# Gated linear attention: gate scan one step later, a third x buffer, and a reordered prologue

## What is computed

```python
q = feature_map((x @ Wq.T) * SCALE); k = feature_map(x @ Wk.T); v = x @ Wv.T   # 16 heads of 16
gate = sigmoid(x @ Wg.T + bg)                                                  # one per token and head
def step(S, inp):
    q_t, k_t, v_t, g_t = inp
    S = g_t[:, :, None, None] * S + k_t[..., :, None] * v_t[..., None, :]
    y_t = einsum('bhi,bhij->bhj', q_t, S)
    return (S, y_t)
y = scan(step)                                                                 # over 1024 tokens
x = layernorm(x + y @ Wo.T)
```

## Time and profile before

| | us |
|---|---|
| runs of the kernel before | 1459.67, 1451.2, 1449.83 |
| their median | 1451.2 |
| the profiled execution, its own time | 1458.73 |
| its span, first to last instruction | 1456.9 |
| mean granted TensorE clock, as a share of full speed | 0.966 |
| PE busy / DVE busy / ACT busy over the whole span | 1357.9 / 790.0 / 582.5 |

### The profile page before, as it was taken

The page is one execution under the profiler, slowest core; times in us unless marked ns, Lnnn a source line. Parts: engine busy times, 40 slices in busy tenths (PEclk is TensorE's granted clock), DMA queues, the critical chain, the costliest instruction groups (busy, mean ns, idle before and its releaser), DMA issues. The chain is left out here.

```text
span 1456.9 us, 22495 instructions
## 1 busy us (share of the span) xinstructions
PE 1357.9 (93%) x7690; PEld 861.7 (59%) x7691; DVE 790.0 (54%) x1539; ACT 582.5 (40%) x1280; POOL 299.8 (21%) x345
## 2 busy tenths in 40 slices
PE   7888999889999999999999997889999999899996
PEld 4555666665555566666666664446665564577774
DVE  4887888866443122222222222467778656676764
ACT  5466666752110122222222221144443532566665
POOL 1133333311673000000000001622220000234343
PEclk9898999979999999999999999899999999999998
DMA  4654555729221011111111112313110000000001
GB/s 143 210 191 167 194 194 195 236 72 347 104 101 50 22 47 47 43 43 47 47 43 43 45 48 62 109 36 98 29 30 0 1 0 12 0 1 16 29 16 58
DMA packets 76741, 115.83 MB, mean 80 GB/s; under 512 B 10032, under 2 KB 62576, under 8 KB 72560
## 3 DMA queue, kind: packets, MB, share of 16 engines
q1 hardware_dynamic: 70096, 97.89, 20.3%
q0 software_dynamic: 6144, 16.79, 3.6%
q10 hardware_dynamic: 416, 0.03, 0.0%
HBM read 82.86 MB, written 31.82 MB: 79 GB/s over the span
## 5 line engine op out<-in xcount | busy, mean ns | idle before, releaser
L1698 POOL DMA_INDIRECT m_got<-outs,slot x64 | 61.2, 956 | 562.1 <-DMA outs<-XT 454.1
L1103 DVE TENSOR_TENSOR ro_h<-ro_bB,ro_sl 128x512 f32<-128x512 f32 x71 | 49.1, 692 | 220.3 <-PE ro_bB L1052 220.3
L548 DVE TENSOR_TENSOR_SCAN a_dcy<-a_gbc,a_ident 128x2048 f32<-128x2048 f32 x32 | 141.6, 4425 | 4.6 <-DMA a_gbc<-gd 0.9
L2054 POOL TENSOR_TENSOR q_hr<-q_hf,q_hr 128x512 fp32r<-128x512 f32 x64 | 83.5, 1315 | 287.6 <-ACT q_hr L1895 287.6
L1047 PE MATMUL ro_bA<-Win,ro_xT 128*128 x284 | 136.4, 603 | 0.8 <-ACT ro_xT L1074 0.6
L1059 PE MATMUL ro_bO<-Wout,ro_hT 128*128 x568 | 134.3, 379 | 0.9 <-DVE ro_hT L1096 0.9
L1059 PEld LDWEIGHTS ro_bO<-Wout,ro_hT 128*128 128x128 f32 x568 | 107.8, 190 | 45.6 <-issue 34.6
L1052 PE MATMUL ro_bB<-Wsw,ro_xT 128*128 x284 | 134.7, 597 | 0.0
L1083 ACT ACTIVATE XT<-ro_bO 128x256 f32<-128x256 f32 x71 | 27.3, 384 | 204.9 <-PE ro_bO L1059 204.9
L1096 DVE COPY ro_hT<-ro_bH 128x512 f32<-128x512 f32 x71 | 49.1, 692 | 101.3 <-PE ro_bH L1032 101.3
L1052 PEld LDWEIGHTS ro_bB<-Wsw,ro_xT 128*128 128x128 f32 x284 | 54.6, 192 | 69.0 <-issue 69.0
(11 more groups left out here) (270 smaller groups left out, 2519.1 us busy)
## 6 DMA issues: line engine op xcount, KB each, us to landing
a_gbc<-gd SPq DMA_DIRECT2D x32, 1024.0 KB, 5.7
rows<-a_zero SPq DMA_DIRECT2D x8, 1152.0 KB, 8.9
XT<-rows SPq DMA_DIRECT2D x71, 128.0 KB, 2.0
outs<-XT SPq DMA_DIRECT2D x71, 128.0 KB, 1.7
a_xt<-in_xTt SPq DMA_DIRECT2D x8, 512.0 KB, 3.8
X<-in_x SPq DMA_DIRECT2D x8, 512.0 KB, 7.5
Win<-in_w_in SPq DMA_DIRECT2D x8, 512.0 KB, 10.5
Wsw<-in_w_sw SPq DMA_DIRECT2D x8, 512.0 KB, 10.4
```

The lines of the kernel that those rows point to most:

```text
L548: v.tensor_tensor_scan(dcy[:, :], gbc[j % 2][:, :], ident16[:, :], 0.0, ALU.mult, ALU.add).then_inc(d_done, 1)
L1698: pool.indirect_dma_start(out=got[q % 2][k][:, t, :], out_offset=None, in_=mem["outs"], in_offset=bass.IndirectOffsetOnAxis(ap=slot[:, k, ...
L2054: pool.tensor_tensor(hr[:, 1, f % 4, :], hf[f % 2][:, :], hr[:, 0, f % 4, :], ALU.subtract).then_inc(hl_done, 1)
```

## The change

The DVE's `gate_decay(n // 4 + 1)` moves from steps n % 4 == 0 to steps n % 4 == 1, and on SP the `gates_out` and `decays_out` of that chunk move with it, now behind `gates_in` and `decays_in` of the step. x has three buffers instead of two, so `load_x(T)` waits for work on chunk T-3 to end instead of T-2 and stands in another place on SP. In the prologue the two fills that PE's opening matmuls read come first on DVE, those matmuls wait for these two fills alone and are 5 instead of 8, and `decay(0)` runs after `phi(1)` instead of after `phi(3)`.

```diff
-        xt = [sb(f"xt{p}", [P, G, B * P]) for p in range(2)]
+        xt = [sb(f"xt{p}", [P, G, B * P]) for p in range(3)]
...
                 def load_x(T):
-                    if T >= 2:
-                        sp.wait_ge(v_ready, 4 * (T - 1))
-                        sp.wait_ge(z_ready, T - 1)
-                    sp.dma_start(xt[T % 2][:, :, :], io["xTt"][T]).then_inc(xt_in[T % 2], 16)
+                    if T >= 3:
+                        sp.wait_ge(v_ready, 4 * (T - 2))
+                        sp.wait_ge(z_ready, T - 2)
+                    sp.dma_start(xt[T % 3][:, :, :], io["xTt"][T]).then_inc(xt_in[T % 3], 16)
...
                 for n in range(0, NT):
-                    if n % 4 == 0 and n // 4 + 1 < NC:
-                        gates_out(n // 4 + 1)
-                        decays_out(n // 4 + 1)
                     if n + 2 < NT:
                         gates_in(n + 2)
                     if 4 <= n + 2 < NT:
                         decays_in(n + 2)
-                    if n % 4 == 2 and n // 4 + 2 < NC:
-                        load_x(n // 4 + 2)
+                    if n % 4 == 1 and n // 4 + 1 < NC:
+                        gates_out(n // 4 + 1)
+                        decays_out(n // 4 + 1)
+                    if n == 0:
+                        load_x(2)
+                    if n % 4 == 3 and n // 4 + 3 < NC:
+                        load_x(n // 4 + 3)
...
+                pe.wait_ge(init, 2)
+                for _ in range(5):
+                    pe.matmul(bV[:, 0:D], zeros[:, :], zero[:, :], start=True, stop=True)
                 pe.wait_ge(init, 3)
-                for _ in range(8):
-                    pe.matmul(bV[:, 0:D], zeros[:, :], zero[:, :], start=True, stop=True)
...
             def _(v):
+                v.memset(zeros[:, :], 0.0).then_inc(init, 1)
+                v.memset(zero[:, :], 0.0).then_inc(init, 1)
                 for t in vz:
...
-                v.memset(zero[:, :], 0.0).then_inc(init, 1)
-                v.memset(zeros[:, :], 0.0).then_inc(init, 1)
...
-                    if n >= 0 and n % 4 == 0 and n // 4 + 1 < NC:
+                    if n >= 0 and n % 4 == 1 and n // 4 + 1 < NC:
                         gate_decay(n // 4 + 1)
...
-                    if tile(n + 1):
+                    if tile(n + 1) and n >= 0:
                         decay(n + 1)
...
                     if Q < 4:
                         phi(Q)
+                    if Q == 1:
+                        decay(0)
```

More of the change, by code:

```diff
@@ L124, in build_attention @@
             sem(k) for k in ("init", "wg_in", "wqk_in", "wv_in", "wo_in", "cst_in", "x_in", "ex_in"))
-        xt_in, gb_in = [sem("xt_in0"), sem("xt_in1")], [sem("gb_in0"), sem("gb_in1")]
+        xt_in, gb_in = [sem(f"xt_in{p}") for p in range(3)], [sem("gb_in0"), sem("gb_in1")]
         gd_out, ed_out = sem("gd_out"), sem("ed_out")
@@ L241, in project @@
                     if o == 0:
-                        pe.wait_ge(xt_in[T % 2], 16 * (T // 2 + 1))
+                        pe.wait_ge(xt_in[T % 3], 16 * (T // 3 + 1))
                     if Q == 0:
@@ L249, in project @@
                     for g in range(G):
-                        mm = pe.matmul(projected(Q), Wqk[:, g, o * P:(o + 1) * P], xt[T % 2][:, g, :], start=(g == 0), stop=(g == G - 1))
+                        mm = pe.matmul(projected(Q), Wqk[:, g, o * P:(o + 1) * P], xt[T % 3][:, g, :], start=(g == 0), stop=(g == G - 1))
                     mm.then_inc(qk_ready, 1)
                 def gates(T):
-                    pe.wait_ge(xt_in[T % 2], 16 * (T // 2 + 1))
+                    pe.wait_ge(xt_in[T % 3], 16 * (T // 3 + 1))
                     if T == 0:
@@ L258, in gates @@
                         for g in range(G):
-                            mm = pe.matmul(bY[32 * b:32 * b + 32, Z0:Z0 + P], WgT[:, g, :], xt[T % 2][:, g, b * P:(b + 1) * P],
+                            mm = pe.matmul(bY[32 * b:32 * b + 32, Z0:Z0 + P], WgT[:, g, :], xt[T % 3][:, g, b * P:(b + 1) * P],
                                            start=(g == 0), stop=(g == G - 1))
@@ L271, in values @@
                     for g in range(G):
-                        mm = pe.matmul(bV[:, 0:D], xt[T % 2][:, g, b * P:(b + 1) * P], Wv[:, g, :], start=(g == 0), stop=(g == G - 1))
+                        mm = pe.matmul(bV[:, 0:D], xt[T % 3][:, g, b * P:(b + 1) * P], Wv[:, g, :], start=(g == 0), stop=(g == G - 1))
                     mm.then_inc(v_ready, 1)
```

## The result

The changed kernel takes 1431.16 us (median of four runs, 1429.67 to 1432.45), the kernel before 1452.48 us (1449.83 to 1459.67): a ratio of 0.984, 95% interval 0.9813 to 0.9868. The forecast was 1421, range 1409 to 1439, with 0.85 on faster. The profiled execution took 1432.45 us in place of 1458.73, 26.3 us less.

A forecast was written before the change was run, and what follows sets the result against it. Bound: in attention, DVE's 26.6 us of waits for ACT's sigmoid of the gates. Gains of 26.0 (chunks) and 6.6 (prologue) sum to 32.6; 28.6 to 32.6 off the 1451.2 median gives 1421 us, range 1409 to 1439.

The forecast's parts named there:

- detour of 3.08 us: ACT's table loads around the sigmoid in gate steps: stays, costs PE 0, with 3.08 a chunk as far end.
- Rival 1: ACT becomes the bound in gate steps, its table detour landing on PE: 1439 in full, 1430 for half; chance 0.14.
- rival 3: The gate broadcast of tile 4k+4 lands too late: slower, 1472 at a 20 us landing; chance 0.04.
- Rival 4: Waits only change names in gate steps; only x waits (5 us) and prologue (6) are won: 1440; chance 0.07.
- the scan and its memset, 0.54 us: On DVE, returning behind weigh in the step after the gate step: 0.54 counted in full, making that step 8.5.
- The last chunk: Chunk from step 24, no gate step behind it and projections ending: forecast 32.1 us.
- the discount of up to 4 us: Chunk 8's late x, perhaps absent in other executions: gain from the median taken as 28.6 to 32.6.
- the prologue: Kernel opening: earlier gates and decay(0) bring step 4's state update from 65.35 to 58.7, gain 6.6 us.
- the 3.3 us of the early gates: Opening: gates run at 5.6 instead of 9.21; 3.3 taken, 0.4 under 3.6 for the lower clock level.
- the bounds of 5 and 7.5: Range of the opening's 6.6 us gain, from the two ends of the early-gates estimate.
- the 4.6 of the clock's second look: Opening: with fewer matmuls first projections may run at half speed, scores(0) 2 us later; gain 4.6 for 6.6.
- Shifts as a whole: The 1131.9 us behind attention hold nothing of the change and only move earlier, unchanged in length.

The follow-up runs named there:

- scan only: Kernel before with only the gate scan and its way out moved one step later; two x buffers, old prologue: 1435.57 us, ratio 0.9867.
- buffers only: Kernel before with only the third x buffer and the new places of the x loads; old scan and opening: 1450.66 us, ratio 0.9986.
- opening only: Kernel before with only the new prologue (early fills, five matmuls, decay(0) behind phi(1)): 1453.16 us, ratio 0.9997.
- scan and opening: Changed kernel with the two old x buffers and the old place of the x loads: 1451.27 us, ratio 0.9881 to the kernel before on its chip.

## Why the prediction was right, and where it was off

The forecast of 1421 was 30.2 us below the median that it started from, and 21.3 were measured: inside the range, on its slow side, and faster by the prediction's own line of 1436.7.

**The bound.** Right. The wait of DVE for the sigmoid was the limit, and moving the scan took it away: scan only gains 16.9 us. The detour of 3.08 us on ACT costs PE nothing: in step 24 the `keep_x` for which `router` waits starts at 233.83, and `router` at 234.34, without a wait; PE waits for ACT only in the last steps, in both kernels. Rival 1 did not come. Neither did rival 3: landings of the gate broadcasts take 4.3 to 8.6 us, and DVE waits for one only in the opening. Rival 4 named prices for the wrong parts: buffers only wins 1.9 us in the medians, and the opening alone nothing.

**The term that was mis-sized: "the scan and its memset, 0.54 us".** It was the length of the instructions at the old place. At the new place the scan starts while POOL adds, and the six scans behind U4 take 0.71, 1.14 and four times 1.40 to 1.42 us, 5.0 us above six of 0.42. The step from U24 takes 9.6 us where 8.5 was forecast; the other three of a full chunk take 7.9, 8.4 and 8.7, against 7.9, 8.3 and 8.9. That POOL and DVE exclude each other stood in the trace of before, at a row that I did not bring in: the decay scan at 245.86 takes 4.42 us, and beside it, in POOL's timeline,

```profile
245.99 4.28 POOL L644 TENSOR_TENSOR a_na<-a_na,a_nt 128x4 f32<-128x4 f32 x1
```

an instruction on 128x4 elements. Sixteen of its 21 records in attention take 0.20 us, and the five of 4.28 start within 0.2 us of the start of a decay scan. So the row showed an instruction held for the whole of a scan, and the place for the gate scan had to be compared with POOL's timeline. In step 24 of before the add ran from 254.22 to 255.48 and the scan from 256.41, by luck behind it. The Trainium skill, "SBUF — State Buffer", SBUF: two separate sides, states this rule: the port pair that DVE and GpSimd share is an exclusive lock for a whole instruction, taken by DVE instructions with two SBUF inputs against a GpSimd instruction that reads SBUF. All rows here agree, also those of the instructions with a PSUM operand, which keep their length beside an add.

**The last chunk.** The prediction priced the chunk from step 24 at 32.1 us, without the 0.54 of a scan, because no gate step follows it. But a scan stands in it, in step 25, for the last chunk's gates. It took 33.83 us in place of 32.1: 0.54 for the scan and its memset, 1.0 for its being held, the rest within 0.2.

**The sum.** Forecast U4 to U28 199.2, measured 205.3: 5.0 for the held scans, 0.54 for the forgotten one, and 0.6 that I do not place. With the 6.3 at U4 for 6.6, the profiled gain is 26.3 where 32.6 was forecast, and attention ends at 300.66, not near 294. To the medians there is a further step. The profiled execution of before lay 6.3 above its median and that of after 1.3, so 21.3 is left; the discount of up to 4 us had to be 5.0. A wait for x that varies from execution to execution would explain it: the profiled ones of before and of scan only, with two buffers, were the second slowest and the slowest of their kernels, and that of buffers only among its fastest. But those of opening only and of scan and opening, with two buffers too, lay in the middle of theirs. Timed runs leave no trace, so this stays open.

**The prologue: the right number for the wrong reason.** U4 came 6.3 us earlier and I had written 6.6 beside "the prologue". But scan only has U4 at 59.11 with the old opening, and the opening alone leaves it at 66.01. The whole gain came with the scan's place: U1 is 2.2 us earlier in scan only, since in step 0 DVE no longer waits 3.47 us for the sigmoid of chunk 1; the step from U1 takes 1.2 less, since DVE does not wait 0.91 us for a broadcast there and PE's `scores` takes 1.15 us again and not 2.09; and step 4, itself a gate step where DVE had waited 1.76 us for the sigmoid, gives 2.8. The prediction's own sum had it so without saying so. It lets `turn_k(0)` end at 27.1 where it had ended at 27.18, so that the 3.3 us of the early gates have run out there, and what it wins behind that point is the wait that stood in step 0 and step 4 before. That the label was wrong and the number right is luck; the bounds of 5 and 7.5 and the 4.6 of the clock's second look all move with the gates, and so had no ground.

Inside the prologue the step that failed is the 6.6 us from the start of `scores(0)` to the end of `turn_k(0)`. `weigh(0)` no longer waits for the decay matrix, as said, but it now waits for `scores(0)` (2.28 us): after an idle time of 6.64 us PE ran it at a granted clock of 0.50, the lower level, 2.09 us for 1.15, and the gates behind it took 1.10. That used up what was saved on x (0.8 us), and the stretch took 7.4 us as before. `phi(3)` was done at 19.91 instead of 20.5, which hid most of it. By the rule that the prediction took from the Trainium skill, "TensorE: Matmul & The Clock Gate", What's actually happening (throttled by default, lifted by activity), the first projections could be slow with five matmuls. They took the same 7.13 us as with eight, and 7.13 to 7.32 in the other runs with five. Without any they were slow, and even that did not reach the path.

**The rest.** "Shifts as a whole" held in the pair of profiles on which the result rests, 1130.0 us in both. On the other two chips the rest is 6 to 18 us longer, for every kernel, and on the third it was longest where attention ended earliest (1139.5, 1143.4, 1147.8 for ends at 300.35, 296.36, 295.09), but also 1147.0 for an end at 303.78. Whether the block behind gives part of an earlier start back, or the executions differ by themselves, stays open. In that block PE waits 5.6 and 6.3 us for ACT on the third chip in the two versions with the scan behind `weigh_k` and 5.6 in the one without opening matmuls; it does not in the two profiles of the changed kernel.

## What to carry to other kernels

Before moving a short instruction to a place where its inputs are ready, lay that place beside GpSimd's timeline, and take the instruction's length from there: in these traces a VectorE instruction with two SBUF inputs and an add on GpSimd did not run together, and one with a PSUM input ran beside it. When a forecast term comes out right, undo that part alone before believing it: here 6.3 us that had been put down to the opening belonged to the scan. Of parts that remove different waits on one path, judge each beside the others: the third buffer is worth 0.14% alone and 0.3 to 0.7% once the sigmoid is out of the way.

## What the runs showed of the hardware

A VectorE instruction with two SBUF inputs that comes while a GpSimd add with two SBUF inputs runs does not share with it: the gate scan, which starts 0.14 us into the add, ends about 0.3 us behind it, 1.40 us for 0.42. It works the other way round too, and costs GpSimd more: in the opening of the changed kernel an add that takes 1.27 us started 0.07 us behind a decay scan of 4.43 us and took 5.43, 1.07 us beyond the scan's end.

```profile
28.05 4.43 DVE L551 TENSOR_TENSOR_SCAN a_dcy<-a_gbc,a_ident 128x2048 f32<-128x2048 f32 x1
28.12 5.43 POOL L630 TENSOR_TENSOR a_qk<-a_eb,a_rb 128x512 f32<-128x512 f32 x1 [19.21 <-ACT a_eb L414]
```

The length of an opening of matmuls on zeros changed from execution to execution at the same code: eight matmuls took 5.20 to 6.72 us, five 4.25 to 4.63, and with 4.63 the gates behind them took 0.95 to 1.10 us in place of 0.66. By the length of the records the lower clock level still held there, but the granted clock of these stretches reads 1.00 in the profiles of before, of the changed kernel and of the one without opening matmuls. Of the opening it is the length of the records that tells.
